# A low-rank and feature-mixing residual kernel: buffers at multiples of 512 bytes, U turned by VectorE, another order in the head

## What is computed

```python
# layer 0: a weight matrix per batch, of rank 30, made from a condition vector
U = (mu @ W_dec + b_dec).reshape(B, 513, 30)        # mu: (2, 256), W_dec: (256, 513*30)
param = einsum('bik,kj->bij', U, V)                 # V: (30, 512)
x = x + (x @ param[:, :-1] + param[:, -1])
# layer 1: six views of x, side by side, through an MLP with a layer norm
h = ln(ln(x, pw_g[path], pw_b[path]), cp_g[comp], cp_b[comp])
t = ln(x, tm_g[time], tm_b[time]);  s = ln(x, ms_g[scale], ms_b[scale])
m, n, r = (x + mlp_ln(state) for the three states)  # one row per batch
w = softmax(aw)
cat = concatenate([w0*h, w1*t, w2*m, w3*n, w4*r, w5*s])        # (.., 3072)
x = x + ln(silu(cat @ int_W1 + int_b1) @ int_W2 + int_b2, int_g, int_be)
```

## Time and profile before

| | |
|---|---|
| three runs | 613.60, 614.84, 614.91 us, median 614.84 |
| the profiled execution | 613.73 us, its span 611.9 us |
| granted TensorE clock | 0.999 of full speed |
| PE busy | 584.0 us, 95% of the span, 2924 matmuls |
| DVE, POOL, ACT busy | 416.7, 389.4, 204.7 us |
| DMA | 102.07 MB, mean 167 GB/s |

### The profile page before, as it was taken

One profiled execution on the slowest core, in us unless ns is written; L12 is line 12 of the kernel. 1 busy time (PEld: TensorE's weight loads), 2 busy tenths in 40 slices (PEclk: granted clock), 3 DMA queues, 4 the chain that ended last, 5 costly groups with the idle time before them and its releaser, 6 DMA issues.

```text
span 611.9 us, 9087 instructions
## 1 busy us (share of the span) xinstructions
PE 584.0 (95%) x2924; PEld 453.9 (74%) x2924; DVE 416.7 (68%) x750; ACT 204.7 (33%) x346; POOL 389.4 (64%) x499
## 2 busy tenths in 40 slices
PE   0999889999999999999999999999999999999995
PEld 0455446588888888888888888888888888888784
DVE  4311277688888888888766676676666666667754
ACT  4333454333334333334233223233322332232222
POOL 1011467568888888888676676666677766666720
PEclk9999999999999999999999999999999999999999
DMA  8999996425544555555433334435443333443201
GB/s 333 406 403 364 351 353 231 148 69 159 160 143 142 162 165 164 147 181 159 144 93 125 125 119 143 123 126 142 142 141 113 130 116 123 120 142 116 79 19 51
DMA packets 51039, 102.07 MB, mean 167 GB/s; under 512 B 9646, under 2 KB 22190, under 8 KB 50876
## 3 DMA queue, kind: packets, MB, share of 16 engines
q1 hardware_dynamic: 38496, 59.54, 28.3%
q0 software_dynamic: 12160, 42.04, 22.4%
q10 hardware_dynamic: 348, 0.06, 0.1%
HBM read 93.11 MB, written 8.39 MB: 166 GB/s over the span
## 4 chain that ended last, share of the span: by engine, by line
PE 83%; DMA 8%; DVE 3%; SPq 2%; issue 2%; POOL 2%; ACT 1%; DVEq 0%; POOLq 0%
PE bank L744 22%; PE bank L745 22%; PE bank L746 22%; PE bank L738 8%; DMA ring<-in_W_dec 5%; DMA ring<-in_int_W 3%; PE bank L795 2%; SPq L333 2%; PE bank L732 2%; PE bank L814 1%; PE bank L810 1%; PE bank L805 1%; DMA pwt<-in_pw,idx 1%; DVE bn L1250 1%; PE bank L886 0%
## 5 line engine op out<-in xcount | busy, mean ns | idle before, releaser
L744 PE MATMUL bank<-W,ops 128*128 128x512 f32 x432 | 177.8, 412 | 0.0
L745 PE MATMUL bank<-W,ops 128*128 128x512 f32 x432 | 171.1, 396 | 0.0
L746 PE MATMUL bank<-W,ops 128*128 128x512 f32 x432 | 170.8, 395 | 0.0
L592 ACT ACTIVATE ops<-bank 128x512 fp32r<-128x512 f32 x97 | 57.1, 590 | 154.0 <-PE bank L738 154.0
L744 PEld LDWEIGHTS bank<-W,ops 128*128 128x128 f32 x432 | 81.7, 189 | 25.2 <-issue 8.4
L746 PEld LDWEIGHTS bank<-W,ops 128*128 128x128 f32 x432 | 81.4, 188 | 19.5
L745 PEld LDWEIGHTS bank<-W,ops 128*128 128x128 f32 x432 | 81.7, 189 | 14.7
L1245 DVE TENSOR_TENSOR ops<-bank,ops 128x512 fp32r<-128x512 f32 x97 | 66.2, 683 | 12.5 <-ACT ops L592 12.5
L1250 DVE BATCH_NORM_STATS2 bn<-h 128x6 f32<-128x512 f32 x32 | 22.2, 693 | 55.2 <-POOL h L1082 55.2
L1022 POOL TENSOR_SCALAR ve<-mv 128x1 f32<-128x1 f32 x94 | 31.3, 333 | 38.7 <-DVE mv L1254 35.3
L641 ACT ACTIVATE xhat<-x,nm,rs 128x512 f32<-128x512 f32 x32 | 26.1, 816 | 82.0 <-POOL nm L1035 82.0
(11 more groups left out here) (145 smaller groups left out, 1080.7 us busy)
## 6 DMA issues: line engine op xcount, KB each, us to landing
ring<-in_W_dec SPq DMA_DIRECT2D x16, 960.0 KB, 12.1
x<-in_x SPq DMA_DIRECT2D x32, 256.0 KB
out<-xb SPq DMA_DIRECT2D x31, 256.0 KB
stash<-in_xT SPq DMA_DIRECT2D x30, 256.0 KB, 5.2
ring<-in_int_W SPq DMA_DIRECT2D x4, 1024.0 KB, 9.2
xraw<-in_xT SPq DMA_DIRECT2D x14, 256.0 KB, 2.8
mnr_row<-in_mnr SPq DMA_DIRECT2D x3, 768.0 KB, 7.6
idxrep<-in_rows SPq DMA_DIRECT2D x32, 64.0 KB, 3.8
```

The lines of the kernel that those rows point to most:

```text
L592: nc.scalar.activation(dst.rearrange("p c t -> p (c t)"), bank[:, :], ACT.Copy).then_inc(done, 1)
L744: nc.tensor.matmul(bank[:, :], op[:, HI, c, :], w[:, HI, c, :], start=start and c == 0, stop=False)
L745: nc.tensor.matmul(bank[:, :], op[:, HI, c, :], w[:, LO, c, :], start=False, stop=False)
L746: last = nc.tensor.matmul(bank[:, :], op[:, LO, c, :], w[:, HI, c, :], start=False, stop=stop and c == KC - 1)
```

## The change

Four things are done at once.

1. **Addresses.** The small buffers are placed together, and all large ones start at a multiple of 512 bytes.
2. **U.** W_dec is laid out by the host in the order in which it is used, so that a piece is 7,680 bytes in a row per partition where it was four rows of 1,920. Its columns are permuted so that DVE's transposes of 32x32 blocks (`turn`, straight from PSUM into `UT`) leave every feature on its partition. `evacuate` on ACT and the 16 DMAs of `to_features` are gone. The addition of the bias reads `UT` with a step of 32 elements.
3. **cst.** The constants' load is cut in two: 508 of 1,203 columns come where all came, the other 695 (347 KB) only before block S; the products that use them wait for a new semaphore, picks_in.
4. **Order.** The calls of the head stand in another sequence on all five engines, and in the regular step four things move: PE transposes h behind the product of T, ACT writes h's high part ahead of z's, DVE writes `tt` ahead of `st`, and `out_scaled` and `one_hot` change places with their neighbours.

```diff
+        cursor[0] += -cursor[0] % LINE          # LINE = 4 * P = 512 bytes, at three places
-        Ur = sb_at(at_ur, "Ur", [P, DECW])
+        UT = sb_at(at_ur, "UT", [P, DECW])
...
-                return d["W_dec"][k * P:(k + 1) * P, 0:D * RANK].rearrange("p (c n) -> p c n", c=KC)[
-                    :, :, m * BANK:(m + 1) * BANK]
+                return d["W_dec"][k * P:(k + 1) * P, m, :].rearrange("p (q n) -> p q n", n=BANK)
...
-        def to_features(eng, got, half, rows):
-            eng.wait_ge(u_row, DECS // 2 * (half + 1))
-            at, n = half * P // 2, P // 2
-            load(eng, got, *[(Uf[at:at + n, b, c, :],
-                              Ur[c * Q + b:c * Q + b + 1, at * RANK:(at + n) * RANK].rearrange(
-                                  "o (p r) -> o p r", r=RANK)) for c, b in rows])
...
-                    load(sp, cst_in, (cst[:, :], d["cst"]))
+                    load(sp, cst_in, (cst[:, 0:AT_BL], d["cst"][:, 0:AT_BL]))
...
             load_ring(sp, MLP1)
+            load_pre(NPRE - 2)
+            load_x(Tile(1))
             load_rows(Tile(0))
-            load_pre(NPRE - 2)
-            load_pre(NPRE - 1)
+            load_rows(Tile(1))
             sp.wait_ge(dec_used, slot[BLK_T] + SLOTS + 1)
             load_ring(sp, BLK_T)
+            load_pre(NPRE - 1)
...
+            load(sp, picks_in, (cst[:, AT_BL:CST], d["cst"][:, AT_BL:CST]))
             sp.wait_ge(dec_used, slot[BLK_S] + SLOTS + 1)
             load_ring(sp, BLK_S)
-            load_rows(Tile(1))
             sp.wait_ge(mlp_used, 4)
             load_ring(sp, BLK_H)
-            load_rows(Tile(2))
+            load_x(Tile(2))
             sp.wait_ge(mlp_used, 3)
             load_ring(sp, BLK_W2)
-            load_x(Tile(2))
+            load_rows(Tile(2))
...
+            def turn(m):
+                v.wait_ge(dec_used, 2 * (m + 1))
+                nc.vector.transpose(UT[:, m * BANK:(m + 1) * BANK], u_bank_of(m)[:, 0:BANK]).then_inc(u_row, 1)
...
-            v.wait_ge(u_in_pool, 16 * 3 * KC)
-            v.wait_ge(u_in_act, 16 * KC)
+            v.wait_ge(u_row, DECS)
...
             def first_step():                     # POOL
                 gathers(t2)
                 rstd(0, t1, mv1_ready, r1_ready)
+                h_first(t1)
                 x_low(t2)
-                h_first(t1)
-                rstd(1, t1, mv2_ready, r2_ready)
                 residual(t0)
                 residual(t1)
+                rstd(1, t1, mv2_ready, r2_ready)
```

More of the change, by code:

```diff
@@ L670, in _ @@
             t_high(t1)
+            s_high(t1)
             embedded(t2)
-            s_high(t1)
             h_norm(t1)
             summed_high(VWst, vw_sum, vw_high)
+            x_high(t2.plus(1))
             x_norm(t2)
-            x_high(t2.plus(1))
             evict_part((bt_used, 1), bt_part)
@@ L680, in _ @@
             silu(t0)
+            s_high(t2)
+            h_norm(t2)
             z_high(t0)
+            t_high(t2)
             embedded(t2.plus(1))
-            h_norm(t2)
-            s_high(t2)
-            t_high(t2)
             def step(n):
@@ L903, in _ @@
             t0, t1, t2 = Tile(0), Tile(1), Tile(2)
+            embed(t0)
+            prefill(NPRE - 1, FRONT)
             pe.wait_ge(silu_ready, 1)
             transpose_rows(HIDT, hid, hidT_sum)
-            embed(t0)
-            prefill(NPRE - 1, FRONT)
+            expand(t0)
+            x_half(t0, 0)
             prefill(NPRE - 1, BACK)
-            expand(t0)
             pe.wait_ge(hidT_ready, 3)
             mlp_second(0)
+            pe.wait_ge(ub_ready, 1)
+            nc.tensor.matmul(pSUM[0:C, :], ident[0:C, 0:C], vec, start=True, stop=False)
             embed(t1)
             mlp_second(1)
-            x_half(t0, 0)
+            mlp_second(2)
             transpose_t(t0)
-            mlp_second(2)
-            pe.wait_ge(ub_ready, 1)
-            nc.tensor.matmul(pSUM[0:C, :], ident[0:C, 0:C], vec, start=True, stop=False)
+            transpose_s(t0)
             x_half(t0, 1)
             sum_parts(sel_m, mlp_part, mlp_sum, start=False)
-            transpose_s(t0)
+            expand(t1)
             x_half(t1, 0)
-            expand(t1)
             x_half(t1, 1)
@@ L941, in _ @@
             offset_product()
+            s_product(t1)
             transpose_h(t1)
@@ L952, in _ @@
             transpose_z(t0)
-            embed(t2.plus(1))
             h_product(t1)
@@ L1204, in _ @@
             last.then_inc(lm_ready, 1)
-            for p in range(2, NPRE - 1):
-                pre_low(p)
+            def turn(m):
+                v.wait_ge(dec_used, 2 * (m + 1))
+                nc.vector.transpose(UT[:, m * BANK:(m + 1) * BANK], u_bank_of(m)[:, 0:BANK]).then_inc(u_row, 1)
+            for j in range(2 * DECS):
+                if j % 2 == 1:
+                    turn(j // 2)
+                if j in PRE_AFTER and PRE_AFTER.index(j) + 2 < NPRE - 2:
+                    pre_low(PRE_AFTER.index(j) + 2)
             def one_hot(a):
@@ L1411, in _ @@
             left_of_vec()
+            scaled(t1)
             scale_rows(t1)
-            scaled(t1)
+            h_stats(t1)
             t_split(t1)
+            s_split(t1)
             stacked(t2)
-            h_stats(t1)
-            s_split(t1)
-            h_gain(t1)
             first_sum(t2)
             x_stats(t2)
+            w2_low(0)
+            scaled(t2)
             split_vw()
+            h_gain(t1)
+            w2_low(1)
             scale_rows(t2)
@@ L1424, in _ @@
             split_bt()
-            w2_low(0)
-            w2_low(1)
+            h_stats(t2)
             z_split(t0)
-            scaled(t2)
-            h_stats(t2)
+            t_split(t2)
+            stacked(t2.plus(1))
             one_hot(t2)
+            h_gain(t2)
             one_hot(t2.plus(1))
-            stacked(t2.plus(1))
-            h_gain(t2)
             s_split(t2)
-            t_split(t2)
             def step(n):
@@ L1587 @@
         "mlp_b2": np.repeat(np.stack([L1[f"{m}_b2"] for m in mlps]), B, axis=0),
-        "W_dec": W_dec,
+        "W_dec": W_dec[:, :NDEC].reshape(MU, KC, P // Q, Q, 2, RANK // 2).transpose(0, 1, 4, 2, 5, 3).reshape(MU, DECS, -1),
         "late": np.concatenate([flat(chunks(put(MU, P, *[(0, q * Q, W_dec[:, NDEC:]) for q in (0, 2, 3)]))),
```

127 lines of the change are left out of this document (61 added, 66 removed).

## The result

The changed kernel takes 612.7 us (median of 12 runs, 609.8 to 614.0) against 614.5 (12 runs, 613.6 to 615.3) for the kernel before. The ratio is 0.9969, 95% interval 0.9957 to 0.9982, so it is faster, by 0.3%. The forecast of 613.0 is 0.3 us off. The profiled execution took 612.38 us with a span of 610.6; that of before 613.73 with 611.9.

What follows compares the result with a forecast made beforehand. PE was taken as the bound, idle only in the head; -1.1 - 0.5 - 3.0 + 1.5 + 0.5 + 1.5 = -1.1 us on 613.73 gave 612.6, named 613.0 for the median (611.5 to 615; with rivals 609.3 to 616.0).

Steps and rivals of the forecast that it cites:

- Start and decodes: Head's beginning: W_dec's first pieces land sooner, -1.1 us (-0.8 to -1.2); PE's wait among the decodes goes, -0.5 us.
- U: Behind the decodes: 0.65 us per block transpose, `Ust` whole near 63.6 us instead of 74.4, PE's wait of 1.2 us gone.
- What is late next, up to the low-rank product: Head after U: new PE waits at stash 11 and block H; low-rank product still ends 2.6 us earlier.
- stash 11: Ahead of `expand(t0)`: its load stands behind block T and both tiles' rows; +1.5 us of PE wait (0.5 to 3).
- The end of the head: From the low-rank product's end to the first `second_product`: a chain from bebc on holds it, +1.5 us (0 to 2.3).
- The end of the head is slower: Rival, chance 0.18: that chain meets every lock at full price, +3.3 there, stash 11 at 3; 616.9 us.
- Addresses ... Nothing here depends on the offset, so I take nothing for the engines: All engines: two DVE subtractions at different offsets took 687 and 693 ns, so new addresses were put at nothing.
- The regular steps ... I put them at nothing: Steps behind the head: PE work end to end, no matmul added or removed, so no change.
- The rival of the steps: A regular step could lose 0.1 us in each of 30 steps, +3; given what is left of the chances.
- Aligned transfers are faster: Rival, chance 0.08: transfers after 62.6 us gain some 6% from rows at multiples of 512; 610.8 us.
- All idle of the head goes: Rival, chance 0.22: loads land early, stash 11 costs 0.5, H and the last stretch nothing; -5.0, 608.7 us.
- No difference: Rival, chance 0.12: head waits are exchanged for others of the same size, the start gives nothing; 613.5 us.

Runs made afterwards that it cites:

- the run with x_low first: Changed kernel with POOL's x_low(t2) ahead of h_first(t1) again, as before the change; 611.9 us, ratio 0.9959 to the kernel before.
- the run with the old end: Changed kernel with the old order at the end of the head, from s_product(t1), x_norm(t1), POOL's first step and scale_rows(t1) on; 609.8 us.
- addresses alone: Kernel before with the changed kernel's buffer addresses and nothing else; 609.7 us, ratio 0.9925.
- the run with the moving operands shifted: Changed kernel with W1, W2 and what follows up to cst moved up by 32 bytes, idx placed behind Uf; 620.2 us.
- addresses and U, old order: Kernel before with the new addresses, U's block transposes, the new W_dec layout and the split cst load, every order as before; 610.7 us.
- U alone: Kernel before with U's block transposes, the new W_dec layout and the split cst load, at old addresses and in old order; 615.4 us.

## Why the prediction was right, and where it wasn't

The number was right by luck: two errors of opposite sign cancelled. In the profiled executions the head was forecast 1.1 us shorter and came out 1.9 longer, an error of 3.0; behind it nothing was forecast and 3.2 us were gained. And 613.0 is itself a value between the sum's 612.6 for one execution and the 613.7 that the same sum gives on the median of 614.8.

- **Start and decodes.** The first decode started at 14.32 us where it was 15.57, and the second piece's at 18.14 where it was 19.54: -1.4 for the start, -1.1 forecast with a range to -1.2. In the other profiles with these loads the second piece's decode starts at 18.02 to 18.50, so -1.0 to -1.5. The rate rose from 402 to 417 GB/s, inside the 0 to 6%. PE no longer waits among the decodes. Both terms hold within what a profile repeats.
- **U.** A block transpose of 128x480 took 0.68 us, 0.65 forecast. The Trainium skill ("Vector Engine (DVE) Microarchitecture Reference", 3.8 The reshape front-end and per-opcode configuration) says that it sustains one element per cycle and lane. The trace agrees as far as its rows go: 1.4 ns an element, where DVE's subtraction of 128x512 takes 1.3. The additions with a stepped read took 0.65 us for two where they took 0.48, the "0.3 more" being 0.2. `Ust` was whole at 62.45 us, 63.6 forecast.
- **What is late next, up to the low-rank product.** Forecast was a lead of 2.6 us at its end; it was 2.8 in this profile and 1.9 in that of the run with x_low first. But a part of it isn't what the forecast counted: with the same order at the old addresses the lead is 1.2 (105.09), so 0.7 to 1.6 us of it came with the addresses, which the sum has at nothing. The pieces: the wait around stash 11 came out at 1.7 us (1.0 for its low part, 0.7 for the stack), +1.5 forecast; `h_product(t0)` started at 96.82 after a wait of 0.4, "near 97" and +0.5 forecast. The 1.1 us for ScalarE's copy of prefilled tile 11, now behind block S, I had not named; the closer products and the 0.3 us more at the start are of a size to cover it.
- **The end of the head: this step failed in size.** I took +1.5 (0 to 2.3) for the stretch that took 21.4 us. It took 129.58 - 103.48 = 26.1, so +4.7, above even the rival "The end of the head is slower" (3.3). The chain that I listed is the one that held it, but it began late: POOL had x_low(t2) behind h_first(t1), PE waited 1.70 us for it in `embed(t2)`, and right behind this wait the granted clock fell (0.50 from 107 to 110 us, 0.79 from 104 to 112), so that `expand(t2)`, the x1 of t2 and its rstd (114.50) followed later. Waits are 3.1 us of the stretch where they were 0.9; from the products of `part` to `expand(t2)` PE took 5.2 us (107.00 to 112.21) where it took 3.7, most of that by the lower clock; the last 0.9 of the 4.7 I can't put down to one thing. The run with x_low first shortened the stretch by 1.8 us, the run with the old end by 4.1, and the latter took 2.9 us off the time.
- **"Addresses ... Nothing here depends on the offset, so I take nothing for the engines": this step failed in kind.** It rested on two DVE rows. These were the wrong rows: the engine that bounds the kernel is PE, and its own groups had the answer, `W,ops` at 395 ns beside `W,xop` at 389 in the same steps of the kernel before. What I put at nothing is worth 4.6 to 5.0 us, and it works through PE's spacing of matmuls, for which the sum had no term.
- **"The regular steps ... I put them at nothing".** Right of the order to some 0.03 us: addresses alone give 16.65 with the old order, the changed kernel 16.64. Wrong of the steps as a whole. I named "if the steps change their length" as what would make the prediction wrong; they did. The rival of the steps had been left no chance at all: the five named ones already add up to 1 (0.40, 0.22, 0.08, 0.12, 0.18), and the lines on faster, same and slower count with a rest that isn't there.
- **The rivals.** "Aligned transfers are faster" is right in kind for W_dec and wrong in size. While W_dec flows (20 to 50 us) the rates are:

| W_dec's rows | large buffers 128 bytes past a multiple of 512 | at multiples of 512 | 32 bytes past |
|---|---|---|---|
| 1,920 bytes | 403 GB/s | 406 | |
| 7,680 bytes | 413 and 414 | 422 | 413 |

So the new layout is worth 10 GB/s and the aligned destination another 8 to 9, 2% and not 6%. The last column is the run with the moving operands shifted, which moves the ring by 32 bytes. The layout changes two things at once, the length of a row and where it starts in DRAM (rows 61,560 bytes apart before, pieces of 7,680 now); which of them counts was not told apart. The rule of the Trainium skill ("DMA: Bandwidth & Descriptors", How a descriptor splits into AXI transactions) is that a descriptor that starts off a 256-byte boundary costs extra beats, for bytes that are fetched and not used. The runs show 2% for the address that is written, a side which that rule doesn't name. Little time comes of it: PE is the bound among the decodes. From 61 to 93 us the aligned addresses give 363 GB/s against 352 in the old order and 362 against 364 in the changed one, so no steady gain there. "All idle of the head goes" and "No difference" did not come. "The end of the head is slower" came, by 4.7 us and not 3.3, but with 1.7 us for stash 11 where it had 3, and its time of 616.9 did not.

## What to carry to other kernels

Where PE is the bound, compare the mean times of matmuls of one form that differ only in their operands: a few ns, repeated over hundreds of products, were worth more here (4.6 to 5.0 us) than all idle time of the head behind the first decode (4.4), and the two operands' addresses had to agree modulo 512 bytes for the fast spacing (a difference of 256 was not tried). A gain at the start can be lost at the next producer in line if that doesn't move up as well: here ScalarE's copy of the partial sums stood behind a pass that waited for a transfer, and with it moved up the first OH product came at 120.14 us where it was 121.41. When the time comes out as forecast, still compare milestone by milestone: an error of 3.0 us and one of 3.2 had cancelled. And a milestone of one profile repeats to about a microsecond only, so take the length of a stretch with the same work in it.

## What the runs showed of the hardware that I had not expected

- fp32r matmuls of 128x128 by 128x512 settle to one every 0.227 us when the stationary and the moving operand start at the same offset modulo 512 bytes (0 and 0, 128 and 128), and stay at 0.233 us with differences of 32, 64, 128 and 288 bytes. Behind a group of transposes the first products of an aligned group are still 0.230 apart on average.
- W_dec's transfers with rows of 7,680 bytes flow at 422 GB/s into buffers at multiples of 512 bytes, and at 413 or 414 into buffers 32 or 128 bytes past one; with rows of 1,920 bytes at 406 and 403.
- Behind a PE wait of 1.70 us the granted clock was 0.50 (1.2 GHz) from 107 to 110 us: two matmuls took 1.91 us where they took 1.02, and one 1.42 where 0.47 is usual. With the wait gone the clock was 1.00. It also fell behind the same wait (1.7 us) in the changed kernel with old or shifted addresses (0.70 to 0.80 from 104 to 112 us), and behind one of 2.20 us for `part` in "addresses and U, old order" (0.57 from 86 to 90); but behind one of 2.46 us in "U alone" it stayed at 1.00. So the length of the last wait alone doesn't decide it.
